# A depthwise convolution in sixteen 32x32 tiles of TensorE, with the banks' output phases turned

## The reference

```
out = relu(_qconv(x, w1))                                            # 1x1, 32 -> 192 planes
out = relu(_qconv(out, w2, stride=1, padding=1, groups=PLANES))      # 3x3 depthwise
out = _qconv(out, w3)                                                # 1x1, 192 -> 32
return out + x
```

## Time and profile before

| what | us |
|---|---|
| median of three runs | 419.36 |
| the profiled execution, device time | 420.1 |
| its span, first to last instruction | 418.3 |
| TensorE busy | 381.3 (91%) |
| VectorE busy | 297.2 (71%) |
| ScalarE busy | 234.5 (56%) |
| depthwise convolution, first to last matmul start | 362.8 to 395.8 |

### The profile page before, as it was taken

The page is one execution under the profiler, slowest core; times in us unless marked ns, Lnnn a source line. Parts: engine busy times, 40 slices in busy tenths (PEclk is TensorE's granted clock), DMA queues, the critical chain, the costliest instruction groups (busy, mean ns, idle before and its releaser), DMA issues. The chain is left out here.

```text
span 418.3 us, 8050 instructions
## 1 busy us (share of the span) xinstructions
PE 381.3 (91%) x2878; PEld 275.1 (66%) x2881; DVE 297.2 (71%) x545; ACT 234.5 (56%) x377; POOL 16.8 (4%) x17
## 2 busy tenths in 40 slices
PE   8786899989999899989999999999988499799986
PEld 8564586768768687867878687787856244355532
DVE  5455726994785778479568847956787689867886
ACT  5223643665485366537546753753685498087761
POOL 6000000360000000000000000000000000000000
PEclk9888699999999999999999999999999699999999
DMA  7454233612443351345325234332500000000004
GB/s 252 120 145 112 71 83 82 163 30 70 102 131 88 76 132 54 72 98 148 87 51 131 69 79 105 81 85 60 118 2 3 0 1 0 2 2 3 2 11 190
DMA packets 19533, 32.56 MB, mean 78 GB/s; under 512 B 4528, under 2 KB 11568, under 8 KB 19504
## 3 DMA queue, kind: packets, MB, share of 16 engines
q1 hardware_dynamic: 19504, 32.17, 29.4%
HBM read 11.38 MB, written 2.10 MB: 32 GB/s over the span
## 5 line engine op out<-in xcount | busy, mean ns | idle before, releaser
L691 PE MATMUL sums_ps<-D,w_hl 128*128 128x512 f32 x576 | 142.7, 403 | 9.1 <-DMA D<-D 5.3
L691 PEld LDWEIGHTS sums_ps<-D,w_hl 128*128 128x128 f32 x576 | 108.6, 191 | 44.9 <-DMA D<-D 10.8
L350 ACT ACTIVATE Y<-mix_ps 128x288 f32<-128x288 f32 x120 | 48.9, 411 | 35.3 <-PE mix_ps L782 23.2
L778 PE MATMUL mix_ps<-mix_hl,F_hl 128*128 128x288 f32 x360 | 65.2, 298 | 3.7 <-issue 1.4
L778 PEld LDWEIGHTS mix_ps<-mix_hl,F_hl 128*128 128x128 f32 x360 | 55.0, 190 | 7.8 <-issue 3.7
L307 ACT ACTIVATE r<-sums_ps,bias_sb 64x512 f32<-64x512 f32 x32 | 21.8, 682 | 52.7 <-PE sums_ps L691 52.5
L439 DVE TENSOR_TENSOR r<-mix_ps,r 64x512 f32<-64x512 f32 x16 | 11.1, 693 | 44.5 <-ACT r L315 37.5
L430 DVE CAST D<-r 64x512 fp32r<-64x512 f32 x48 | 19.9, 415 | 28.6 <-ACT r L307 23.0
L782 PE MATMUL mix_ps<-mix_hl,X 96*128 96x288 f32 x120 | 35.3, 298 | 0.0
L967 ACT ACTIVATE q_I<-ps,w_bias 128x1024 f32 x24 | 25.4, 1110 | 16.6 <-PE ps L1198 16.6
L432 DVE TENSOR_TENSOR D<-r,D 64x512 fp32r<-64x512 f32 x48 | 32.9, 685 | 1.6
(11 more groups left out here) (128 smaller groups left out, 473.2 us busy)
## 6 DMA issues: line engine op xcount, KB each, us to landing
D<-D SPq DMA_DIRECT2D x96, 126.0 KB, 2.3
F<-r SPq DMA_DIRECT2D x96, 64.0 KB, 2.0
x_own<-in_x_pads SPq DMA_DIRECT2D x16, 288.0 KB, 3.5
F<-in_x_mix SPq DMA_DIRECT2D x16, 128.0 KB, 2.6
xb<-in_x_res SPq DMA_DIRECT2D x8, 256.0 KB, 2.7
out<-q_res SPq DMA_DIRECT2D x8, 256.0 KB, 2.0
w_raw<-in_w_conv SPq DMA_DIRECT2D x6, 192.0 KB, 4.2
w_raw<-in_w_int SPq DMA_DIRECT2D x1, 843.0 KB, 4.8
```

Source lines behind the costliest of these rows:

```text
L350: nc.scalar.activation(Y[:, u, g], banks(p, u)[:, g % 4, 0:MIX], ACT.Copy).then_inc(y_out, 1)
L691: last = nc.tensor.matmul(conv_ps[u][:, bank, :], w_hl[:, wp, n, d, :], D[f][u][:, xp, :, 4 * d:4 * d + RUN], start=start and d == 0 and h ...
L778: nc.tensor.matmul(y, F_hl[u][:, xp, h, k], mix_hl[:, wp], start=n == 0, stop=False, skip_group_check=True)
```

## The change

The array is used as sixteen 32x32 tiles: one row tile is one input phase, one column tile is 32 output partitions. The work of a set is cut into four turns. In turn t, row tile r computes output phase r xor t, and writes it for column tile c into bank r xor c xor t. So in each turn the four row tiles write four different banks, and each bank has its output phases in another order. A row tile has 4 taps in turn 3, 2 in turns 1 and 2, and 1 in turn 0, and all row tiles have the same number; the turns run in the order 3, 1, 2, 0. Within a turn a round is 16 matmuls with one tap each. All 16 matmuls of the last round of a turn increment `c2_turns`, and the next turn waits until all have done so. Three copies of the last weights, `w3_turned`, take the place of `w3_swap`; GpSimd makes them with twelve copies of 32 columns for each group.

```diff
-            for half in (0, 64):
-                nc.gpsimd.tensor_copy(keep.w3_swap[:, :, half:half + 64], w3[:, :, 64 - half:NP - half])
+            for turn in range(1, 4):
+                for q in range(4):
+                    nc.gpsimd.tensor_copy(keep.w3_turned[:, turn - 1, :, 32 * q:32 * q + 32],
+                                          w3[:, :, 32 * (q ^ turn):32 * (q ^ turn) + 32])
...
-                for n, quarter in enumerate(zip(*(c2_tile(row, col) for row in range(2) for col in range(2)))):
-                    if n in C2_TURNS:
-                        pe.wait_ge(c2_half, sets * 8 + C2_TURNS[n])
-                    for row, col, b, h, pi, u, v, first, final in quarter:
-                        rows = slice(64 * row, 64 * row + 64)
-                        field = q2[rows, par, two + b, 2 * h * FIELD:2 * (h + 1) * FIELD]\
-                            .rearrange("p (m l i) -> p m l i", m=2, i=FS)
-                        at = 4 * (2 * u + v) + 2 * pi
-                        last = nc.tensor.matmul(
-                            ps[64 * col:64 * col + 64, 2 * (two + b) + h],
-                            diag[rows, g, at:at + 2].rearrange("p q c -> p (q c)"),
-                            field[:, :, u:u + PH, v:v + PH], start=first and row == b,
-                            stop=final and row != b, skip_group_check=True)
-                        if final and row == b:
-                            last.then_inc(c2_half, 1)
+                for n, turn in enumerate(C2_TURNS):
+                    if n:
+                        pe.wait_ge(c2_turns, (sets * 3 + n) * 16)
+                    taps = len(c2_taps(0, turn))
+                    for t in range(taps):
+                        for row in range(4):
+                            rows = slice(32 * row, 32 * row + 32)
+                            u, v = c2_taps(row, row ^ turn)[t]
+                            for col in range(4):
+                                b, h = divmod(row ^ col ^ turn, 2)
+                                field = q2[rows, par, two + b, 2 * h * FIELD:2 * (h + 1) * FIELD]\
+                                    .rearrange("p (m l i) -> p m l i", m=2, i=FS)
+                                last = nc.tensor.matmul(
+                                    ps[32 * col:32 * col + 32, 2 * (two + b) + h],
+                                    diag[rows, g, 4 * (2 * u + v) + (row ^ turn)],
+                                    field[:, :, u:u + PH, v:v + PH], start=n == 0 and t == 0,
+                                    stop=n == 3 and t == taps - 1, skip_group_check=True)
+                                if n < 3 and t == taps - 1:
+                                    last.then_inc(c2_turns, 1)
                 last.then_inc(c2_done, 2)
...
-                        w3 = w3_swap[:, g] if b % 2 else w_q[:, W1 + NP * g:W1 + NP * g + NP]
+                        turn = 2 * (b % 2) + h
+                        w3 = w3_turned[:, turn - 1, g] if turn else w_q[:, W1 + NP * g:W1 + NP * g + NP]
...
-def c2_tile(row, col):
...
-    for b, h in ((0, 0), (0, 1), (1, 0), (1, 1)) if row == 0 else ((1, 0), (1, 1), (0, 0), (0, 1)):
-        pi = col ^ b
-        taps = [(u, v) for u in range(2) for v in ((row,) if row == pi else (0, 1))]
-        for n, (u, v) in enumerate(taps):
-            yield row, col, b, h, pi, u, v, n == 0, n == len(taps) - 1
-
-
-C2_TURNS = {4: 2, 8: 6, 10: 8}
+def c2_taps(row, phase):
...
+    pi, pl = divmod(row, 2)
+    ob, oa = divmod(phase, 2)
+    return [(u, v) for u in range(2) for v in range(2) if abs(2 * u - pl - oa) < 2 and abs(2 * v - pi - ob) < 2]
+
+
+C2_TURNS = (3, 1, 2, 0)
```

More of the change, by code:

```diff
@@ L884, in quantised_block @@
     w_q, fields, ident, ones = keep.w_q, keep.fields, keep.ident, keep.ones
-    minus_zero, zero_pt, c2_most, w3_swap, diag = (
-        keep.minus_zero, keep.zero_pt, keep.c2_most, keep.w3_swap, keep.diag)
+    minus_zero, zero_pt, c2_most, w3_turned, diag = (
+        keep.minus_zero, keep.zero_pt, keep.c2_most, keep.w3_turned, keep.diag)
     with ExitStack() as ctx:
@@ L918, in quantised_block @@
         c1_folded, c2_folded, c2_peaks = sem("c1_folded"), sem("c2_folded"), sem("c2_peaks")
-        c2_half = sem("c2_half")
+        c2_turns = sem("c2_turns")
         c1_done, c1_out, c1_out_dve = sem("c1_done"), sem("c1_out"), sem("c1_out_dve")
@@ L1297, in program @@
         keep.c2_most = sb("c2_most", [NP, 2, PX], F16)
-        keep.w3_swap = sb("w3_swap", [NP, NG, NP], BF16)
+        keep.w3_turned = sb("w3_turned", [NP, 3, NG, NP], BF16)
         keep.diag = sb("diag", [NP, NG, 16, C], BF16)
```

## The result

The changed kernel takes 437.59 us (median; 435.83 to 440.52, 4 runs) against 419.65 of the kernel before (4 runs); the ratio is 1.042, interval 1.0377 to 1.0464. It is slower by 17.9 us, where +19.8 was forecast (439 for the median, 439.9 for the profiled execution). The profiled one took 440.52 us with a span of 438.8.

A forecast was written before the change was run, and what follows sets the result against it. TensorE's depthwise matmuls were taken to set the pace, VectorE second. Sets +19.6, tail -0.3 and GpSimd +0.5 made +19.8 us: 439.9 for the profiled execution, 439 for the median, range 426 to 450.

The forecast's parts named there:

- The round of sixteen: Depthwise convolution on TensorE: sixteen 32x32 matmuls beside each other take 0.231 us, as four 64x64 matmuls did before.
- columns set the pace at both neighbours: Reason for 0.231 us a round: the matmuls' columns, not their number, set the time in the two stages compared.
- my upper bound of 0.34 us a round: Depthwise convolution: sixteen matmuls at the cosine transform's 21 ns per weight load and matmul take at most 0.34 us.
- The switch: Between turns: 0.45 to release, 15 further increments of 0.035, 0.03 to the matmul; 1.005 us, three times a set.
- The set and the stage: Depthwise convolution: six plain steps and three waits for the turn before make 4.40 us against 2.77; twelve sets, +19.6 us.
- The tail: End of the depthwise stage: TensorE's end had about 0.3 us of slack before ScalarE and VectorE, used first: -0.3 us.
- GpSimd and the last stage: Twelve copies may delay VectorE's operations beside them, +0.5 us (0 to 2); last pointwise stage's other weight addresses, 0.
- Half clock: Rival, chance 0.08: idle time at switches lowers TensorE's clock, +1.65 us per set; 449 for half the sets, 459 for all.
- Cheap increments: Rival, chance 0.09: waits drain TensorE but increments don't serialise; switch 0.53 us, set 2.98 us, whole 422 us.
- the waits don't bite: Rival, chance 0.05: switches cost as little as plain steps, set 2.08 us, gain stops at 3.9 us: 415.5 us.
- VectorE as the next bound: In the faster rival, VectorE's maxima and quantisations set the depthwise stage's pace and stop the gain at 3.9 us.
- the main case: Drains and serialised increments slow the depthwise stage: 439 us, own range 426 to 447, chance 0.78.

The follow-up runs named there:

- the two parts alone: The kernel before with only w3_turned, its twelve GpSimd copies and its use in the last stage, depthwise convolution unchanged: 419.22 us against 418.76, ratio 1.0010.

## Why the prediction was right, point by point

**The round of sixteen.** Forecast 0.231 us. Measured 0.24 within a turn of two, and (4.28 - 3 x 0.96) / 6 = 0.233 in the mean. Right, but for a reason that was too wide: "columns set the pace at both neighbours" holds while the code is there. Neither nor the earlier trace rows had 256 instructions at that rate one after another, and my upper bound of 0.34 us a round had no term for a stall after every 128 matmuls. Without waits the mean over a stall and its burst is 3.83 / 8 = 0.48 us, outside both bounds.

**The switch.** Forecast 1.005, measured 0.96. The semaphore's updates in the trace of the changed kernel (the round that starts at 400.165 us) give the parts: the first count 0.40 us after the round's first start, sixteen counts 0.034 apart, the next matmul 0.04 behind the last: 0.40 + 15 x 0.034 + 0.04 = 0.95. So 0.035 was right as the distance of two counts, and the 0.05 too much lay in the 0.45 and 0.03. But taking counts away saves less than that distance, since the matmuls of a round end one after another whether they count or not: by one, four and sixteen counts it is 0.026 for each. The Trainium skill ("TensorE: Matmul & The Clock Gate", the per-tile semaphore tail) gives 26.3 ns for an increment; the trace agrees.

**The set and the stage.** Forecast 4.40 and +19.6, measured 4.28 and 12 x 1.51 = +18.1 at full clock. This is where the time went, and TensorE's own counts are what it waited for, 36 times. In the median of the runs +17.9 stands against 18.1 - 0.2 + 0.5 by the measured parts. That the profiled execution came within 0.7 us of its 439.9 is luck: it holds 5.4 us of half clock and a stage that began 3.0 earlier, both outside the sum.

**The tail.** Forecast -0.3: VectorE's reduction at 418.17 waited 1.90 us for ScalarE where before it ran back to back. From the last matmul's start to the last reduction's end it is 420.53 - 416.4 = 4.1 us against 400.11 - 395.8 = 4.3. Right in sign, -0.2.

**GpSimd and the last stage.** Forecast +0.5 within 0 to 2; twelve copies at 0.51 us took 5.6 us, and the two parts alone made +0.46 us, an amount that isn't told from nothing.

**Half clock.** I gave it 0.08, since TensorE would be busy for 61% and a stretch of 56% had kept its clock. In the profiled execution it fell for parts of four sets, with TensorE busy for 64% of the time ahead of them (8.10 of 12.60 us). The step "above what held, so unlikely" was wrong: 64% lost the clock here, and in the last five sets 65% (13.96 of 21.44 us) kept it at 1.00. The price (+1.65 us a set at the lower of the two clocks) was about right: the set that ran wholly at 1.2 GHz took 6.1 us, +1.8. The other three runs had a higher mean clock, 0.972 to 0.977 against 0.956; where in them it fell isn't on record.

**The rivals' prices.** "Cheap increments, 422" and "the waits don't bite, 415.5" would both have been wrong had they come true: 433.5 and 436.4 were measured for these conditions. Both left out the same thing: 3456 instructions in straight line took 47.9 us (one increment) and 50.5 (no waits, 362.0 to 412.5) with TensorE standing still between blocks. VectorE as the next bound, 2.4 us a set, isn't shown either: once the code looped, the last eight sets took 2.33 us each, with TensorE busy for 97% of the time and VectorE for 84%. A slip of the sum: by its own terms (+0.63 us a set) the main case's lower end is 427, not 426.

The changed kernel itself stands near that second limit: 256 of its instructions take 4.28 x 256 / 288 = 3.80 us, and its matmuls never wait for "issue" inside a set. Making its switches cheaper gained 4.1 us at most (433.5), and taking them away 1.2, which isn't told from none. No kernel of this study beats the one before; that one issues 96 instructions in 2.77 us and has waits that ask only for old counts.

## What to carry to other kernels

A wait on the matmuls issued just ahead drains the array: with 512 columns it cost 0.34 us over a plain step at four counts in 64x64 tiles and 0.57 for the whole switch at one count in 32x32, with 0.026 us for each further count. Counts also held back the matmuls behind them where nobody waited. So ask for counts two rounds old, and let one matmul do the counting. When a tiling is refined, count the instructions as well as the rounds: three and four times as many small matmuls in straight line code were bounded by how fast code is brought, at 28 to 29 ns for a weight load with its matmul (47.9 and 50.5 us for 1728). Before trusting a gain from removing one wait, take that wait away in a kernel that may compute something else, and see what stands behind it.

## What the runs showed of the hardware

- TensorE's straight line code came in blocks of 256 instructions, in 32x32 and in 64x64 tiles alike, one each 3.83 us in a stretch without waits; 3456 instructions took 50.5 us without waits and 47.9 with one count a switch; the stall shows as idle time that ended with "issue", after every 127 or 128 matmuls. A loop of 1152 matmul and weight load instructions brought one block of that queue in its second and third pass together, which ran without stalls.
- Sixteen increments at each of three rounds in nine held back the matmuls behind them though nobody waited: 2.5 to 2.6 us for 128 matmuls in place of 2.1 to 2.2. The increments of sixteen tiles stood 0.034 us apart.
- Sixteen 32x32 matmuls of 512 columns ran beside each other at 0.23 us a round.
- The granted clock fell to the lower level after TensorE had been busy for 64% of 12.6 us (8.10 of 12.60), at a granted clock of 1.00 until then; in the same execution it stayed at 1.00 over 21.4 us with TensorE busy for 65%.
- A wait on an instruction of its own, a `sem_inc`, compared with a register, cost 0.09 us more than the wait on the weight load (0.66 against 0.57).
